# LSTM with a chosen cell: the input rows enter the gate sums through TensorE instead of through VectorE

## The reference, cut to what matters

```python
def step(carry, x_t):
    h, c = carry
    sel_in = jnp.concatenate([h, c, x_t], axis=-1)
    logits = sel_in @ W_sel.T + b_sel
    onehot = jax.nn.one_hot(jnp.argmax(logits, axis=-1), 4)
    g_all = einsum('bi,sgi->bsg', x_t, W_ih) + einsum('bh,sgh->bsg', h, W_hh) + b_ih + b_hh
    g = jnp.einsum('bsg,bs->bg', g_all, onehot)     # i, f, g, o of the picked cell
    c = sigmoid(f) * c + sigmoid(i) * tanh(g)
    h = sigmoid(o) * tanh(c)
```

## Time and profile before

| | us |
|---|---|
| median of 3 runs | 6420.35 (6419.92 to 6422.26) |
| the profiled execution | 6423.3 |
| its span, first to last instruction | 6421.3 |
| busy in the span: TensorE, its weight loads, VectorE, ScalarE, GpSimd | 5387.0, 3259.0, 3158.5, 1088.2, 613.4 |
| granted TensorE clock, mean over the span | 0.945 of 2.4 GHz |

### The profile page before, as it was taken

The page is one execution under the profiler, slowest core; times in us unless marked ns, Lnnn a source line. Parts: engine busy times, 40 slices in busy tenths (PEclk is TensorE's granted clock), DMA queues, the critical chain, the costliest instruction groups (busy, mean ns, idle before and its releaser), DMA issues. The chain is left out here.

```text
span 6421.3 us, 214665 instructions
## 1 busy us (share of the span) xinstructions
PE 5387.0 (84%) x84946; PEld 3259.0 (51%) x84948; DVE 3158.5 (49%) x13265; ACT 1088.2 (17%) x4645; POOL 613.4 (10%) x1014
## 2 busy tenths in 40 slices
PE   8997878849989658888888888888888888878778
PEld 6543443324657435555555555555555555544444
DVE  4402443214541365555555555555555555555543
ACT  0000000012321131111111111111111111122312
POOL 0000750003630000000000000000000000001100
PEclk9998989979999879999999999999999999989877
DMA  0000111566433400000000000000000000000010
GB/s 10 26 26 10 40 41 39 120 173 209 120 97 130 182 16 5 10 5 5 5 5 10 5 5 5 5 5 10 5 5 5 5 10 0 0 23 36 14 62 8
DMA packets 128787, 240.28 MB, mean 37 GB/s; under 512 B 47084, under 2 KB 64114, under 8 KB 127687
## 3 DMA queue, kind: packets, MB, share of 16 engines
q1 hardware_dynamic: 68584, 146.72, 6.5%
q0 software_dynamic: 60128, 92.58, 5.7%
HBM read 165.58 MB, written 73.29 MB: 37 GB/s over the span
## 5 line engine op out<-in xcount | busy, mean ns | idle before, releaser
L1457 PE MATMUL bank<-lstm_w,step_h_parts 128*32 128x128 f16 (+1 forms) x59904 | 1229.7, 237 | 327.8 <-issue 327.8
L1457 PEld LDWEIGHTS bank<-lstm_w,step_h_parts 128*32 128x32 f16 x59904 | 1109.1, 97 | 648.4 <-issue 634.5
L1427 PE MATMUL bank<-lstm_w 128*128 128x512 f16 x4992 | 1296.7, 382 | 3.3 <-issue 3.3
L1481 DVE TRANSPOSE_TENSOR_REDUCE step_summed<-bank 128x4 f32<-128x128 f32 x1872 | 670.6, 358 | 299.5 <-PE bank L1457 278.9
L1427 PEld LDWEIGHTS bank<-lstm_w 128*128 128x128 f16 x4992 | 386.3, 98 | 388.8 <-issue 5.1
L1406 ACT ACTIVATE step_act_out<-step_gates 128x4 f32<-128x4 f32 x625 | 128.6, 206 | 2124.2 <-DVE step_gates L1487 2120.8
L1534 DVE COPY step_xgs<-step_xg 128x16 f32 x624 | 109.0, 175 | 731.1 <-issue 705.3
L1487 DVE SCALAR_TENSOR_TENSOR step_gates<-step_summed,lstm_inv_scale,step_xgs 128x4 f32<-128x4 f32 x1872 | 414.9, 222 | 64.8
L1396 POOL COPY xnT<-step_state 128x4 f32 (+1 forms) x625 | 116.5, 186 | 3317.3 <-DVE step_state L1514 3317.3
L1109 PE MATMUL bank<-sum_parts,sum_hot 125*125 125x512 f16 x1600 | 347.6, 381 | 6.7 <-DVE sum_parts L1068 6.7
L1437 PE MATMUL bank<-lstm_wsel,step_state 128*1 128x4 f32 x4992 | 214.9, 168 | 110.7 <-DVE step_state L1504 110.7
(11 more groups left out here) (368 smaller groups left out, 6617.4 us busy)
## 6 DMA issues: line engine op xcount, KB each, us to landing
rel_h<-rel_h_sb SPq DMA_DIRECT2D x39, 1024.0 KB, 4.3
lstm_xg<-xg_g POOLq DMA_DIRECT2D x4, 5000.0 KB, 19.5
step_xg<-lstm_xg SPq DMA_DIRECT2D x25, 800.0 KB, 4.4
xg_w<-in_c_w_ih SPq DMA_DIRECT2D x8, 2048.0 KB, 10.8
lstm_w<-in_c_w_hh SPq DMA_DIRECT2D x4, 4096.0 KB, 31.0
rel_z<-rel_z_sb POOLq DMA_DIRECT2D x8, 1250.0 KB, 22.9
rel_zg<-rel_z POOLq DMA_DIRECT2D x8, 1248.0 KB
cheb_w<-in_L_gnn_weight SPq DMA_DIRECT2D x8, 1024.0 KB
```

Source lines behind the costliest of these rows:

```text
L1427: nc.tensor.matmul(idle[:], w[:, 0, 0, 0, 0, 0:128], w[:, 0, 0, 0, 0, :], start=True, stop=True)
L1457: last = nc.tensor.matmul(bank[32 * q:32 * q + 32, 0:32 * (end - first)], h_parts[:, c, :], w[:, s, c, q, a, 32 * first:32 * end], start=( ...
L1481: nc.vector.tensor_reduce(summed[:, first:end], bank[:, 0:32 * (end - first)].rearrange("p (b r) -> p b r", r=32), X_AXIS, ALU.add, apply_ ...
```

## The change

The input rows of all four cells now enter the gate sums on TensorE.

1. `lstm_inputs` computes rows of time steps instead of rows of gates: 80 tiles of 125 steps by 512 gate values. Each is split into three bf16 parts (VectorE three operations, ScalarE two) and stored by POOL's queue as soon as it is done. The bias now lies along the free dimension, so 8,192 values are loaded into each of 125 partitions, twice, and added there.
2. `lstm_steps` holds 48 partitions of such parts (16 groups, three parts each), 5 steps a chunk, 15 in the ring. At the head of each step TensorE puts them into four gate banks with one product of 128x512 each (`inject`), all four cells side by side in a bank. A matrix of ones and zeros, scaled as the weights are, sends the three parts of a group to one row.
3. The cell's 128 matmuls of 128 columns (parts f, g, i, o with 32 each) add to the picked cell's quarter of each bank. VectorE reduces that quarter, at an address that it computes from the pick, and ScalarE applies the scale within its activation. L1487's additions, L1534's copy and WARM_GATES are gone.
4. VectorE's loop begins with the choice: its branch back now stands between the last operation on `h` and the maximum.

```diff
+            sp.dma_start(w[:, 0], I["c_w_ih"][0]).then_inc(w_loaded[0], 16)
+            sp.dma_start(b_ih[:].rearrange("p g d -> p (g d)"), I["c_b_ih"].rearrange("(a d) -> a d", a=1).to_broadcast((R, 8192))).then_inc(b_loaded, 16)
+            sp.dma_start(b_hh[:].rearrange("p g d -> p (g d)"), I["c_b_hh"].rearrange("(a d) -> a d", a=1).to_broadcast((R, 8192))).then_inc(b_loaded, 16)
...
+            for i in range(TILES):
+                n, m = i // NT, i % NT
+                pool.wait_ge(lo_ready, i + 1)
+                pool.dma_start(B.xg[n, :, m * R:(m + 1) * R, :].rearrange("a t g -> t a g"), parts[:, i % 4]
+                               ).then_inc(stored[i % 4], 16)
...
+            def take(i):
+                if i >= 4:
+                    dve.wait_ge(lo_ready, i - 3)
+                dve.wait_ge(done, i + 1)
+                nc.vector.tensor_tensor(value[:, i % 4], B.bank[i % 6][0:R, :], b_ih[:, i // NT], ALU.add
+                                        ).then_inc(value_ready, 1)
+
+            def take_rest(i):
+                dve.wait_ge(hi_ready, i + 1)
+                nc.vector.tensor_tensor(value[:, i % 4], value[:, i % 4], parts[:, i % 4, 0], ALU.subtract
+                                        ).then_inc(rest_ready, 1)
+
+            def take_lo(i):
+                dve.wait_ge(mid_ready, i + 1)
+                nc.vector.tensor_tensor(parts[:, i % 4, 2], value[:, i % 4], parts[:, i % 4, 1], ALU.subtract
+                                        ).then_inc(lo_ready, 1)
...
+            for i in range(TILES + 2):
+                if i < TILES:
+                    take(i)
+                if 1 <= i <= TILES:
+                    take_rest(i - 1)
+                if i >= 2:
+                    take_lo(i - 2)
```

```diff
+                act.wait_ge(summed_f, n)
+                nc.scalar.activation(act_out[:, 0:4], summed[:, 0:4], ACT.Sigmoid, scale=L.inv[:, 0:1]
+                                     ).then_inc(sig_f, 1)
...
+            def inject(part, at, stop):
+                p, bank, _, _ = part
+                return nc.tensor.matmul(bank[:], rows[:, p, :], xg[:, at], start=True, stop=stop)
+
+            def add_half(part, s, c, a, stop):
+                p, bank, _, _ = part
+                for q in range(4):
+                    last = nc.tensor.matmul(bank[32 * q:32 * q + 32, 128 * s:128 * s + 128], h_parts[:, c, :],
+                                            w[:, s, c, q, a, 128 * p:128 * p + 128], start=False, stop=stop,
+                                            tile_position=(0, 32 * q))
+                return last
...
+                pe.wait_ge(xg_loaded, (t // XG_CHUNK + 1) * 16)
+                at = bass.ds((t % XG_RING) * 512, 512)
+                for part in parts:
+                    pe.wait_ge(part[3], t)
+                    last = inject(part, at, stop=False)
+                last.then_inc(injected, 1)
...
+                    for part in parts:
+                        for c, a in halves:
+                            last = add_half(part, s, c, a, stop=(c == KC - 1 and a == 1))
+                        last.then_inc(part[2], 1)
...
-                keep_clock_up(WARM_GATES)
...
-            def add_rows(part, t):
-                first, end, bank, done, summed_part, _ = part
-                dve.wait_ge(done, t)
-                nc.vector.tensor_reduce(summed[:, first:end], bank[:, 0:32 * (end - first)].rearrange(
+            def add_rows(part, s, n):
+                p, bank, done, summed_part = part
+                dve.wait_ge(done, n)
+                nc.vector.tensor_reduce(summed[:, 4 * p:4 * p + 4], bank[:, bass.ds(s * 128, 128)].rearrange(
                     "p (b r) -> p b r", r=32), X_AXIS, ALU.add, apply_transpose=True).then_inc(summed_part, 1)
...
-                s = dve.value_load(pick[0:1, 0:1], min_val=0, max_val=CELLS - 1)
-                dve.wait_ge(xg_loaded, (t // CHUNK + 1) * 16)
-                nc.vector.tensor_copy(xgs[:], xg[:, bass.ds(s, 1), bass.ds((t % RING) * GC, GC)]
...
+                return dve.value_load(pick[0:1, 0:1], min_val=0, max_val=CELLS - 1)
...
+                add_rows(part_f, s, n)
+                add_rows(part_g, s, n)
                 forget(n)
-                add_input(part_ig, t)
-                add_rows(part_o, t)
+                add_rows(part_i, s, n)
+                add_rows(part_o, s, n)
                 new_i(n)
-                add_input(part_o, t)
-                dve.wait_ge(h_kept, t)
...
+            nc.vector.memset(xg[:], 0.0).then_inc(cleared, 1)
...
+            with dve.Fori(1, STEPS) as t:
+                s = choose(t)
+                finish(s, t, t + 1)
```

More of the change, by code:

```diff
@@ L1359, in lstm_steps @@
+    w = L.raw[:, 0:BLOCKS, :].bitcast(F16).rearrange("p (s c q) (a k) -> p s c q a k", s=CELLS, c=KC, a=2)
+    part_f = (0, B.bank[0], done_f, summed_f)
+    part_g = (1, B.bank[1], done_g, summed_g)
+    part_i = (2, B.bank[2], done_i, summed_i)
+    part_o = (3, B.bank[3], done_o, summed_o)
+    parts = (part_f, part_g, part_i, part_o)
+    score = B.bank[4][0:1, 0:8]
+    idle = B.bank[5]
+    halves = [(c, a) for c in range(KC) for a in range(2)]
     with ExitStack() as here:
-        xg = sb("xg", [128, CELLS, RING * GC], F32)
@@ L1361, in lstm_steps @@
[L1361 removed]
+        xg = sb("xg", [128, XG_RING * 512], BF16)
+        rows_f = sb("rows_f", [128, GATES, 128], F32)
+        rows = sb("rows", [128, GATES, 128], BF16)
         state = sb("state", [128, 8], F32)
@@ L1452, in cell @@
                 def cell(s):
-                    for first, end, bank, done, _, _ in parts:
-                        for c in range(KC):
-                            for a in range(2):
-                                for q in range(4):
-                                    last = nc.tensor.matmul(
-                                        bank[32 * q:32 * q + 32, 0:32 * (end - first)], h_parts[:, c, :],
-                                        w[:, s, c, q, a, 32 * first:32 * end],
-                                        start=(c == 0 and a == 0), stop=(c == KC - 1 and a == 1),
-                                        tile_position=(0, 32 * q))
-                        last.then_inc(done, 1)
+                    for part in parts:
+                        for c, a in halves:
+                            last = add_half(part, s, c, a, stop=(c == KC - 1 and a == 1))
+                        last.then_inc(part[2], 1)
                 with pe.If(s < 2):
@@ L1556, in _ @@
             dve.wait_ge(init, 1)
-            dve.wait_ge(xg_loaded, 16)
-            for first, end, _, _, _, gates_part in parts:
-                nc.vector.tensor_copy(gates[:, first:end], xg[:, 0, first:end]).then_inc(gates_part, 1)
-            forget(1)
-            new_i(1)
-            new_c(1)
-            weigh_h(1)
-            new_h(1)
-            choose(1)
-            with dve.Fori(1, STEPS - 1) as t:
-                finish(t, t + 1)
-                choose(t + 1)
-            finish(STEPS - 1, STEPS)
+            dve.wait_ge(rows_loaded, 16)
+            nc.vector.tensor_scalar(rows[:], rows_f[:], L.up[:, 0:1], None, ALU.mult).then_inc(rows_ready, 1)
+            finish(0, None, 1)
+            with dve.Fori(1, STEPS) as t:
+                s = choose(t)
+                finish(s, t, t + 1)
 def add_hidden(nc, ctx, B, L):
@@ L2291, in lay_out @@
         b = out.pop("L2_ffn_" + name).reshape(4, 4, 4, 4, 32)[:, order]
-        out["c_" + name] = np.ascontiguousarray(b.transpose(2, 4, 0, 1, 3).reshape(128, 64))
+        out["c_" + name] = np.ascontiguousarray(b.transpose(1, 2, 0, 3, 4).reshape(8192))
+    rows = np.zeros((128, 4, 128), np.float32)
+    for n in range(16):
+        rows[3 * n:3 * n + 3, n // 4, 32 * (n % 4)] = 1.0
+    out["c_xg_rows"] = rows
     w = out.pop("L2_ffn_W_sel")
```

184 lines of the change are left out of this document (83 added, 101 removed).

## The result

| | us |
|---|---|
| before, median | 6421.31 (6419.92 to 6422.92) |
| changed kernel, median of 4 runs | 6642.42 (6635.89 to 6649.44) |
| ratio | 1.034, 95% interval 1.033 to 1.036 |
| its profiled execution's span | 6634.1 (before: 6421.3) |
| predicted | 6552, range 6425 to 6680 |

The changed kernel is 221 us slower; 132 were forecast. The span of the profiled execution, the fastest of its four, grew by 212.8 us. The start of the first and of the last index (FIND_INDEX8) of the loop divide it in three. Ahead of the first: 2307.2 us before, 2390.9 now, **+83.7** (forecast +12). Between them, 623 steps: 3370.8 before, 3498.9 now, **+128.1** (forecast +120). Behind the last: +1.0. So the loop came as worked out, and the stage ahead of it did not.

The account below looks back on a forecast made before the run. It took the chain within a step, with TensorE's exposed loop turn, as the bound: 6423.3 + 120 (loop) + 12 (outside) = 6555 us for an execution like the profiled one, 3.0 above the median, so 6552 us, range 6425 to 6680.

Parts of the forecast that it names:

- The ring through TensorE and its turn: Loop step: cell, TensorE's now uncovered loop turn, injects and logits in one chain; a step grows by 0.24 us.
- Cell 3 loses nothing: Loop steps that pick cell 3: no jump at its end, so its 129 steps lose only about 0.01 us each.
- VectorE waits 0.3: Loop step: VectorE's gain is not seen; its maximum could start at 4020.40, but TensorE's logits come at 4020.74.
- Outside the loop +12: Input-row stage about +4 (from -5 to +30), loop's start +6, first pass through longer code +2: +12 us.
- TensorE's columns (+6.5): Input-row stage: columns grow from 64 x 4 x 625 to 80 x 4 x 512, 2.4% of 272 us.
- The loop's start (+6): Ahead of the loop: clearing 3,840 words a partition (4 us) and making the first gates through TensorE, +6 us.
- A wait of about 5: Input stage's start: two 4,000 KB broadcasts and an addition precede the first freed bank; six banks cover 21 us.
- The last store is small: -4: Input stage's end: last store 375 instead of 5,000 KB, but the inputs' logits chain now ends the stage; -4 us.
- The turn stays hidden: Rival: injects start by 4018.75, the ring closes over VectorE 0.10 us a step earlier, 6370 us; chance 0.10.
- The instruction memory: Rival: cells of 1,024 TensorE instructions no longer stay in instruction memory, one miss a step, 8,700 us; chance 0.04.
- The clock: Rival: TensorE, standing still between cell and injects, runs a third of the time at half clock, 7,100 us; chance 0.03.
- The stage ahead: Rival: each broadcast reads the same 32 KB 125 times; at a quarter of the rate, +60 or more us; chance 0.03.

Follow-up runs that it names:

- e1_early: The changed kernel with the four products that put in the input rows moved from the loop's head to its end, ahead of TensorE's branch back: 6504.57 us.
- e6_one_more: The changed kernel with one more 128x512 product, which nobody reads, right behind the four that put in the input rows: 6776.54 us.
- e7_nowarm: The kernel before without the four idle products at the loop's end (WARM_GATES = 0), nothing else: 6765.14 us, ratio 1.053.

## Why the prediction was right, and where it failed

**The total: inside the range, in part by luck.** The loop is 8 us over its forecast and all outside it 73. The rest of the 90 us is the distance of the two profiled executions from the medians of their kernels' runs. The upper bound allowed 100 us for slower register operations and 18 for the stage ahead; the first went unused and covered what the second lacked. One of its signs of being wrong, "a stage ahead that is over 30 us longer", came.

**The ring through TensorE and its turn: right.** Counted from the first cell product, in us, forecast and measured: last cell product 1.75 and 1.75; first row product 2.57 and 2.53; logits' first product 3.53 and 3.50; those of c 3.58 and 3.61; those of h 3.78 and 3.82; maximum 4.23 and 4.27. A step of cell 0 was to be 5.50 and is 5.53. The sum of the register operations and the wait was put at 0.44; from the first of them (4017.40) to the first row product are 0.39. The one term that was off is the distance from the input's logit product to those of c: put at 0.05, and 0.11 here. No row showed 0.05: in the earlier trace rows the two stand 0.36 apart, with a wait for c between them. Less the row products' early start of 0.04 that leaves 0.03 a step in cells 0 to 2, 15 us; cell 3, 0.03 shorter on the mean where +0.01 was put, gave back 5. That makes 10 us, where the loop missed by 8. e1_early shows that the turn, not the products, was the cost, and e6_one_more that TensorE's chain is the end of every step.

**Cell 3 loses nothing: right.** No jump on its path: the first row product stands 2.31 behind the first cell product there, in the others 2.53. Against its undisturbed steps before it loses 39 ns; the -62 of the others is the pause behind the eighth matmul that went, which the prediction did not have.

**VectorE waits 0.3: right in kind.** L1561 was to start 3.49 behind the first cell product and does at 3.55; the maximum waits 0.54, of which VectorE's branch, ending at 4019.12 by its sequencer's rows (L1599), takes a quarter.

**"Outside the loop +12": wrong, by 73 us.** The steps of that sum, one by one. TensorE's columns (+6.5) came as +2: 80 tiles of eight products, one each 0.43, are 274 where there were 272. It started 7.3 earlier (1900.18, before 1907.49), where 4 was put. The loop's start (+6) is right: from its first DMA to the first index 12.1 us, before 6.8. "A wait of about 5" is what failed: it was 47.8. The sum took the broadcasts to move at about the rate of the weights. They do not: 1930 to 1960, when nothing else moves, has a DMA share of 0.31 and 135 GB/s, and the weights of the next stage, 2280 to 2315, have 1.00 and 433 GB/s. 0.31 is 5 of 16 engines, and with 5 and 16 at work each moves 27 GB/s in both rows. The broadcasts fill 125 partitions and the weights 128. The Trainium skill, "DMA: Bandwidth & Descriptors", section "Why a DMA increments its semaphore by 16 and not by 1", says that a DMA runs on the largest number of engines, at most 16, that divides the outermost size on both sides; for 125 that is 5, and the trace agrees with both rows. The prediction's own reason for a slow broadcast, that it reads the same 32 KB 125 times, falls by another row: the store of `x` at the program's end takes 1,250 KB, each row once, from 125 partitions, and runs alone:

```profile
6627.00:6629.00 2.00, 0.00 (x0) 0.00 (x0) 0.00 (x0) 0.00 (x0) 0.00 (x0) 0.50 0.33 128
```

The trace of the kernel before has the same 0.33 and 128 GB/s there (6412 to 6416), so the rate could have been read ahead of the forecast. The broadcasts in another number of partitions were not tried. At 135 GB/s the 8,000 KB (8.19 MB) take 61 us, and the rival's 60 would have been the forecast.

"The last store is small: -4" failed too. It counted the last store and not the 79 ahead of it. Each lands 8.6 us after its issue, four may be on the way, and a tile comes each 3.43 us; with those waits in the chain of value, high part, rest, middle part and store, the 75 tiles from 1968.0 to 2241.4 took 3.65 us each, 16 us more than TensorE's own, and the stage's end came 35.4 us behind TensorE's last tile, where it had been 18.5, 17 us more: 33 us together. The cover for VectorE's three operations that the text named was there; what was not asked is how long ScalarE's copies wait for a buffer.

**The rivals.** The turn stays hidden: the first row product came at 2.53, 0.20 behind the point (2.33) from which that decides. The instruction memory: one instruction packet falls between 2400 and 5800 us, as before (now at 2401.5, in the loop's first steps), so the cells' 1,024 instructions, products and weight loads, ran without a fetch a step. The clock: 1.00. The prediction called the idle products cover for the turn, and put a fall of the clock at 550 us with a chance of 0.03, without a row for either; in the kernel before, with nothing in their place, the clock does fall, for 342 us (e7_nowarm). The stage ahead, with a chance of 0.03, came true beside the forecast and not in its stead: chances that add to one hide that two of the cases can hold together.

## What to carry to other kernels

A branch and register arithmetic cost nothing here while the array had queued work to run over them: put that work ahead of the branch, not behind it, and look at what stands behind the last wait before you move anything there. When one engine's turn is uncovered, the other's is worth nothing to hide; it is worth it afterwards (at most 5 us, then 88). Before calling products idle, run the kernel without them, and before costing a transfer, read the DMA share of a row with the same number of partitions.

## What the runs showed that was not expected

- Four products of 128x512 in a step of 5.26 us that nobody reads hold the granted clock at 1.00. Without them it goes back and forth between 1.00 and 0.50 (0.85 over 200 us), though TensorE never pauses longer than 0.88 us, and the kernel is 5.3% slower.
- Those four cost no time at all where they stand: steps at the full clock have the same length without them.
- A transfer into 125 partitions moved 135 GB/s at a DMA share of 0.31, one into 128 partitions 433 GB/s at 1.00. A store from 125 partitions without a broadcast moved 128 GB/s at 0.33.
- From the start of the cell's last product to the start of the first one behind the jump, the loop's branch and two register operations are 0.78 us, and the array is idle for 0.56 of them.
